# A macaron transformer layer: the context is turned by VectorE's 32x32 transposes, x1 is made as columns, and work and places move between engines

## What is computed

```python
# ffn, D=128, 16 heads of 8, 8 experts, 512 hidden
x = conv1d(x, conv_w, width 3) + conv_b
q, k, v = split(x @ wqkv.T + bqkv)
ctx = softmax(q @ k.T / sqrt(8)) @ v          # 512x512 scores for each of 16 heads
x = layernorm(x + ctx @ wo.T + bo, ln1_g, ln1_b)
probs = softmax(x @ gate_w + gate_b)          # over 8 experts
y_e = relu(x @ w1[e] + b1[e]) @ w2[e] + b2[e] # every expert on every token
x = layernorm(x + sum_e probs[e] * y_e, ln2_g, ln2_b)
# attn: per head a softmax over the 16 steps of a segment and offset of q*k, times v, then Wo
```

## Time and profile before

| | us |
|---|---|
| median of 3 runs | 1628.72 |
| lowest and highest | 1626.53 and 1637.02 |
| the profiled execution | 1626.09 |
| its span, first to last instruction | 1624.4 |
| TensorE busy | 1557.1 |
| VectorE busy | 1184.1 |
| ScalarE busy | 1151.7 |
| GpSimd busy | 981.6 |

### The profile page before, as it was taken

The page is one execution under the profiler, slowest core; times in us unless marked ns, Lnnn a source line. Parts: engine busy times, 40 slices in busy tenths (PEclk is TensorE's granted clock), DMA queues, the critical chain, the costliest instruction groups (busy, mean ns, idle before and its releaser), DMA issues.

```text
span 1624.4 us, 26990 instructions
## 1 busy us (share of the span) xinstructions
PE 1557.1 (96%) x8690; PEld 871.0 (54%) x8690; DVE 1184.1 (73%) x1885; ACT 1151.7 (71%) x1684; POOL 981.6 (60%) x925
## 2 busy tenths in 40 slices
PE   3889999999999999999999999999999999999986
PEld 2334555555555555555655555555555555555565
DVE  3766677776777778777778786878787777768365
ACT  2566777777777777677676776777677677777875
POOL 3512657676766667566675766667566676757143
PEclk7678999999999999999999999999999999999998
DMA  7533333151522424243331523425243331511111
GB/s 191 142 82 88 83 81 95 49 130 40 127 64 74 104 70 121 53 116 80 85 96 47 150 54 80 105 72 120 53 112 83 83 96 46 133 35 47 28 46 26
DMA packets 85853, 137.52 MB, mean 85 GB/s; under 512 B 8977, under 2 KB 49602, under 8 KB 81090
## 3 DMA queue, kind: packets, MB, share of 16 engines
q1 hardware_dynamic: 84434, 131.60, 31.7%
q0 software_dynamic: 1280, 4.20, 1.0%
HBM read 102.73 MB, written 32.77 MB: 83 GB/s over the span
## 4 chain that ended last, share of the span: by engine, by line
PE 82%; DVE 5%; DMA 4%; issue 3%; POOL 3%; ACT 2%; SPq 0%; POOLq 0%; DVEq 0%; ACTq 0%
PE hid_y L997 15%; PE ctx_ps L1178 14%; PE hid_y L1001 12%; PE hid_y L998 12%; PE score L1035 11%; DMA m_xn<-out 2%; PE misc L997 2%; PE misc L998 2%; PE misc L1001 2%; DVE negmax L847 1%; PE score L1055 1%; DMA f_xn<-in_L_attn_x 1%; PE misc L1102 1%; PE misc L1123 1%; PE misc L1109 1%
## 5 line engine op out<-in xcount | busy, mean ns | idle before, releaser
L559 POOL TENSOR_TENSOR hidl<-hid,hidh 128x512 fp32r<-128x512 f32 x456 | 590.2, 1309 | 342.5 <-DVE hidh L806 256.6
L847 DVE TENSOR_REDUCE negmax<-score 128x2 f32<-128x1024 f32 x484 | 590.4, 1220 | 224.9 <-PE score L1035 222.9
L673 ACT ACTIVATE probs<-score 128x1024 f32<-128x1024 f32 x468 | 480.6, 1027 | 107.3 <-PE score L1055 106.9
L702 ACT ACTIVATE hid<-hid_y,cols 128x512 f32<-128x512 f32 x484 | 332.1, 686 | 149.3 <-PE hid_y L1001 130.8
L1178 PE MATMUL ctx_ps<-probs,V 128*18 128x512 f32 x2048 | 275.6, 611 | 0.0
L1055 PE MATMUL score<-Qp,Kp 32*128 32x512 f32 (+1 forms) x1024 | 269.0, 505 | 2.6 <-ACT probs L666 2.4
L1035 PE MATMUL score<-Kp,Qp 24*128 24x512 f32 x968 | 245.1, 501 | 22.4 <-DVE negmax L847 9.5
L997 PE MATMUL hid_y<-x1h,w1h 128*128 128x512 f32 x484 | 230.9, 477 | 1.6 <-DVE negmax L847 1.3
L567 POOL TENSOR_TENSOR yacc<-yacc,gated 128x512 f32<-128x512 f32 x128 | 180.5, 1410 | 67.5 <-DVE gated L822 67.5
L699 ACT ACTIVATE hidh<-hid_y,cols 128x512 fp32r<-128x512 f32 x256 | 175.7, 686 | 51.6 <-PE hid_y L1001 49.8
L997 PE MATMUL hid_y<-hidh,w2h 128*128 128x512 f32 x512 | 206.3, 403 | 4.4 <-DVE gated L822 4.4
(11 more groups left out here) (184 smaller groups left out, 1893.1 us busy)
## 6 DMA issues: line engine op xcount, KB each, us to landing
gate_b<-gate_dram SPq DMA_DIRECT2D x128, 256.0 KB, 3.7
q_parts_dram<-q_parts SPq DMA_DIRECT2D x48, 256.0 KB, 3.0
k_parts_dram<-k_parts SPq DMA_DIRECT2D x48, 256.0 KB, 3.0
Qp<-q_parts_dram SPq DMA_DIRECT2D x64, 192.0 KB
Kp<-k_parts_dram SPq DMA_DIRECT2D x64, 192.0 KB
Qp<-q_parts_dram SPq DMA_DIRECT2D x32, 240.0 KB
Kp<-k_parts_dram SPq DMA_DIRECT2D x32, 240.0 KB
Qp<-q_parts_dram SPq DMA_DIRECT2D x32, 144.0 KB
```

Source lines behind the costliest of these rows:

```text
L559: pool.tensor_tensor(hidl[:, n % RING, :], hid[:, n % 2, :], hidh[:, n % RING, :].bitcast(F32), ALU.subtract).then_inc(s["h_lo"], 1)
L673: act.activation(probs[:, n % 2, 2 * j:2 * j + 2, :], score2[:], ACT.Exp, scale=SCALE)\
L702: act.activation(hid[:, n % 2, :], hid_bank(u, n), ACT.Relu, bias=col(n))\
L847: dve.tensor_reduce(negmax[:, g % 2, :, k % 8], banks_for_max(u.count(32, k))[:], AX.X, ALU.max, negate=True).then_inc(s["a_max"], 1)
```

## The change

Eight edits, and a new `AT`:

1. `ctx_ps` is turned by VectorE in 32x32 blocks (`dve.transpose`, one instruction per half), from PSUM to `ctxT`. Reciprocals and scaling work on `ctxT`, and one product over 256 elements takes the place of two over 128. A third `dve.transpose` turns `ctxs` back to `ctxT`. TensorE's 12 transposes and ScalarE's 3 copies go. The columns of `wo` and of the value bias are loaded in another order for it.
2. x1 is made as columns: one product with `woT` as weights and 512 columns of `ctxT`. VectorE adds the bias (now a column, `bo_col`) and `conv` in one instruction. Four transposes (`x1T`) bring it back to rows, and the moments and the centring read `misc`.
3. `yacc` is evicted by ScalarE behind `x1h`, no longer by VectorE.
4. `nm_parts` is turned by `pe.transpose`.
5. The gates are turned in one transpose of 32 columns, and stored as 32 rows of 128.
6. GpSimd centres and scales `f_xn` (units after the first) and `m_xn`, and multiplies `m_xn` by `mwt`.
7. The start loads `wo` in four pieces and the value bias in two, adds `bo2` to the columns, and drops one broadcast: five more DMAs.
8. `AT` has new places: the context's first turn from tick 56 (copy) to 59.5, `f_v` from -7 to -6, x1 from 97.5 to 93.5, the c moments from 100 to 94.5, and others by up to 5 ticks.

```diff
@@ AT
-    "f_k1": -23, "f_k2": -23, "f_qs": -24, "f_ks": -21.5, "f_v": -7, "f_vs": -7, "ctx0": 56, "ctx0T": 59.5,
-    "ctx0n": 60.5, "ctx1": 88.5, "ctx1T": 90.5, "ctx1n": 90.5, "cT": 94.5, "cTs": 94.5, "x1": 97.5, "x1p": 98,
+    "f_k": -23, "f_k1": -23, "f_k2": -23, "f_qs": -25, "f_ks": -22, "f_v": -6, "f_vs": -6, "ctx0": 59.5,
+    "ctx1": 89, "cT": 90.5, "x1": 93.5, "x1p": 92.5, "x1T": 94.5, "c_stats": 94.5, "c_centre": 95.5, "c_rs": 95,
...
@@ misc_uses
-            + [misc_use("ctx0T", "a_norm", 2, 1), misc_use("ctx1T", "a_norm", 2, 2), misc_use("cT", "c_cTs", 1, 1),
-               misc_use("x1", "c_x1p", 1, 1), misc_use("xnT", "c_x1h", 1, 1), misc_use("gate", "c_lg", 1, 1),
+            + [misc_use("x1", "c_x1p", 1, 1), misc_use("x1T", "c_cen", 1, 1), misc_use("xnT", "c_x1f", 1, 1), misc_use("gate", "c_lg", 1, 1),
...
@@ SyncE, start
-            load(wo_raw, wo, "ld_wo")
+            load(vec_rows[V_BO:V_BO + 1, :], row(bo2), "ld_vec")
+            for j in range(HG):
+                half, pair = divmod(j, 2)
+                load(wo_raw[:, 32 * j:32 * j + 32],
+                     wo[:, 64 * half:64 * half + 64].rearrange("o (g i d) -> o i g d", i=2, d=DH)[:, pair, :, :], "ld_wo")
...
@@ GpSimd
+                if T == AT["f_centre"] and u.n > 0:
+                    centre(pool, "f", u.n, f_xn)
+                if T == AT["f_norm"] and u.n > 0:
+                    normalise(pool, "f", u.n, f_xn, "f_xn")
...
+                if T == AT["m_centre"]:
+                    centre(pool, "m", b.n, m_xn)
                 if T == AT["m_rs"]:
                     inv_std("m", b.n)
+                if T == AT["m_norm"]:
+                    normalise(pool, "m", b.n, m_xn, "m_xn")
+                if T == AT["m_w"]:
+                    wait(pool, s["m_wt"], b.count(1, 1))
+                    pool.tensor_tensor(by_offset(m_xn[:]), by_offset(m_xn[:]), over_steps(mwt), ALU.mult)\
+                        .then_inc(s["m_w"], 1)
...
@@ ScalarE
-                if T in CTX_EVICT:
-                    g = CTX_EVICT[T]
-                    wait(act, s["a_pv"], u.count(16, 8 * g + 8))
-                    wait(act, s["a_ctxT"], u.count(2, g))
-                    wait(act, s["c_x1"], u.n)
-                    act.activation(ctxT[:], ctx_ps[:], ACT.Copy).then_inc(s["a_ctx"], 1)
...
-                if T == AT["cTs"]:
-                    wait(act, s["c_cT"], u.count(1, 1))
-                    act.activation(ctxT[:], misc[:], ACT.Copy).then_inc(s["c_cTs"], 1)
                 if T == AT["x1h"]:
-                    wait(act, s["c_x1f"], u.count(1, 1))
+                    wait(act, s["c_xnT"], u.count(1, 1))
...
+                    wait(act, s["e_T"], u.n - 1)
+                    act.activation(yacc[u.parity][:], misc[:], ACT.Identity, bias=col(V_B1), scale=col(V_G1))\
+                        .then_inc(s["c_x1f"], 1)
...
@@ VectorE
-                if T in CTX_NORM:
-                    g = CTX_NORM[T]
...
+                if T in CTX_TURN:
+                    g = CTX_TURN[T]
+                    wait(dve, s["a_pv"], u.count(16, 8 * g + 8))
+                    wait(dve, s["zero_ctx"], 1)
+                    wait(dve, s["c_x1T"], u.n)
+                    dve.transpose(ctxT[:], ctx_ps[:]).then_inc(s["a_ctx"], 1)
+
+                    sums = ctxT[:].rearrange("p (b r) -> p b r", r=QUARTER)[:, :, 0:2 * VC]\
+                        .rearrange("p b (l v) -> p b l v", v=VC)
+                    means = ctxs[:].rearrange("p (b t l d) -> p b t l d", t=2, l=2, d=DH)
+                    wait(dve, s["a_ctx"], u.count(2, g + 1))
+                    dve.reciprocal(rden[:], sums[:, :, :, DH]).then_inc(s["a_rden"], 1)
                     wait(dve, s["a_rden"], u.count(2, g + 1))
...
+                    dve.tensor_tensor(means[:, :, g, :, :], sums[:, :, :, 0:DH],
+                                      rden[:].unsqueeze(3).to_broadcast([128, S // QUARTER, 2, DH]), ALU.mult)\
+                        .then_inc(s["a_norm"], 1)
+                if T == AT["cT"]:
+                    wait(dve, s["a_norm"], u.count(2, 2))
+                    dve.transpose(ctxT[:], ctxs[:]).then_inc(s["c_cT"], 1)
 
                 if T == AT["x1p"]:
                     wait(dve, s["c_x1"], u.count(1, 1))
+                    wait(dve, s["set_bo"], 2)
+                    dve.scalar_tensor_tensor(out=ctxT[:], in0=misc[:], scalar=bo_col[:], in1=conv[u.parity][:],
+                                             op0=ALU.add, op1=ALU.add).then_inc(s["c_x1p"], 1)
...
@@ TensorE
-                    pe.matmul(misc[0:2 * HG * TC, 0:128], nm_parts[:].rearrange("p t a k -> p (t a k)").bitcast(F32),
-                              ident[:], start=True, stop=True).then_inc(s["a_nmT"], 1)
...
+                    pe.transpose(misc[0:2 * HG * TC, 0:128],
+                                 nm_parts[:].rearrange("p t a k -> p (t a k)").bitcast(F32), ident[:])\
+                        .then_inc(s["a_nmT"], 1)
+                if T == AT["x1"]:
...
+                    wait(pe, s["c_cT"], u.count(1, 1))
+                    pe.matmul(misc[:], woT[:], ctxT[:], start=True, stop=True).then_inc(s["c_x1"], 1)
+                if T == AT["x1T"]:
...
+                    wait(pe, s["c_x1p"], u.count(1, 1))
                     for c in range(TC):
                         last = pe.transpose(chunk(misc, c), chunk(ctxT, c), ident[:])
-                    last.then_inc(s["a_ctxT"], 1)
...
-                    for c in range(TC):
-                        pe.matmul(chunk(misc, c), chunk(ctxT, c), woT[:], start=True, stop=False)
-                        last = pe.matmul(chunk(misc, c), chunk(conv[p], c), ident[:], start=False, stop=True)
-                    last.then_inc(s["c_x1"], 1)
+                    last.then_inc(s["c_x1T"], 1)
...
-                    for c in range(TC):
-                        last = pe.transpose(misc[0:E, c * 128:(c + 1) * 128], gate[p][:, c, :], ident[:])
-                    last.then_inc(s["c_prT"], 1)
+                    pe.transpose(misc[0:TC * E, 0:128], gate[p][:].rearrange("p c e -> p (c e)"), ident[:])\
+                        .then_inc(s["c_prT"], 1)
```

More of the change, by code:

```diff
@@ L368, in _ @@
             load(vec_rows[V_CONV:V_CONV + 1, :], row(conv_b), "ld_vec")
-            load(vec_rows[V_BQ:V_BQ + 3, :], bqkv.rearrange("(a n) -> a n", a=3), "ld_vec")
+            load(vec_rows[V_BQ:V_BQ + 2, :], bqkv[0:2 * D].rearrange("(a n) -> a n", a=2), "ld_vec")
+            for half in range(2):
+                load(vec_rows[V_BV:V_BV + 1, 64 * half:64 * half + 64],
+                     bqkv[2 * D + 64 * half:2 * D + 64 * half + 64].rearrange("(g i d) -> i g d", i=2, d=DH), "ld_vec")
             for k, v in ((V_G1, ln1_g), (V_B1, ln1_b), (V_MBQ, bq), (V_MBK, bk), (V_MBV, bv)):
@@ L874, in tick @@
-                if T == AT["c_stats"]:
-                    wait(dve, s["c_x1p"], u.count(1, 1))
-                    moments("c", u.n, lambda c: chunk(x1n, c))
-                if T == AT["c_centre"]:
-                    centre("c", u.n, x1n)
-                if T == AT["c_norm"]:
-                    normalise("c", u.n, x1n, "c_xn")
-                if T == AT["x1f"]:
-                    wait(dve, s["c_xnT"], u.count(1, 1))
-                    wait(dve, s["e_T"], u.n - 1)
-                    dve.tensor_scalar(yacc[u.parity][:], misc[:], col(V_G1), col(V_B1), ALU.mult, ALU.add)\
-                        .then_inc(s["c_x1f"], 1)
+                    wait(dve, s["set_bo"], 2)
@@ new lines, in tick @@
+                    dve.scalar_tensor_tensor(out=ctxT[:], in0=misc[:], scalar=bo_col[:], in1=conv[u.parity][:],
+                                             op0=ALU.add, op1=ALU.add).then_inc(s["c_x1p"], 1)
+                if T == AT["c_stats"]:
+                    wait(dve, s["c_x1T"], u.count(1, 1))
+                    moments("c", u.n, lambda c: chunk(misc, c))
+                if T == AT["c_centre"]:
+                    wait(dve, s["e_x"], u.n - 1)
+                    centre(dve, "c", u.n, x1n, misc)
@@ L973, in mid @@
                                       ALU.mult).then_inc(s["m_wt"], 1)
-                if T == AT["m_w"]:
-                    wait(dve, s["m_wt"], b.count(1, 1))
-                    dve.tensor_tensor(by_offset(m_xn[:]), by_offset(m_xn[:]), over_steps(mwt), ALU.mult)\
-                        .then_inc(s["m_w"], 1)
                 if T == AT["m_o"]:
```

149 lines of the change are left out of this document (59 added, 90 removed).

## The result

Kernels are timed side by side. The changed kernel has a median of 1589.8 us in 4 runs (1583.9 to 1598.3), the kernel before 1632.9 (1626.5 to 1643.7): a ratio of 0.9756, 95% interval 0.9715 to 0.9797. The forecast was 1600, range 1582 to 1617.

A forecast was written before the change was run, and what follows sets the result against it. TensorE was taken as the bound, full in the steady part, with VectorE nearly failing to keep up. From the profiled 1626.1: - 43 + 12 + 1.5 + 1 = 1597.6 us, against the median 1600; range 1582 to 1617.

The forecast's parts named there:

- TensorE's saving: Fewer transposes and products on TensorE: 1.14 + 0.94 - 0.38 + 0.96 + 0.25 = 2.9 us per unit, 43 us over 15 units.
- nothing gained, or 0.96: Bounds on the gain per unit in us from turning the maxima by transposes, forecast as 4 x 0.24 = 0.96.
- The wait at the first half: At the context's first half TensorE waits for VectorE's turn, reciprocals and scaling: 0.8 us per unit, 12 us in all.
- The c norm's 1.5 us: Moments, cast and centring between two maxima, directly after x1T, make it about 0.1 us late: 15 x 0.1.
- The mids: GpSimd's three more passes in each of 8 mids were costed at nothing; without cover, up to 1.3 us each.
- the cover: GpSimd's passes are hidden because a down projection reads its `hidl` about five ticks after GpSimd's place for it.
- The start: Five more DMAs issued ahead of the rest, at 0.36 us each: at most 1.8 us, taken as 1.
- Rival 1: The wait at the first half doesn't come, because VectorE reaches it earlier: 1586 us, chance 0.22.
- Rival 2: VectorE or GpSimd later than counted (slow turns, collisions, late `m_xn`, no maxima gain): one 1608 to 1614, chance 0.25.
- Rivals 3 and 4: The third: maxima hold TensorE over the whole unit, time 1620 to 1635, chance 0.06. The fourth has its own line.
- rival 4: Slower: VectorE becomes the bound through its turns, at the second half; 1656 us for turns of 2.44, chance 0.04.
- the recorded point: Where VectorE's turns outweigh the gain: from 28 us, 1.9 per unit, that is from turns of 1.5 us on.

## Why the prediction was right, and where its terms were off

**The sum.** By the profiled executions the forecast was 28.5 us less, and 27.8 was measured. By the medians it was 28.7, and 43.1 was measured, 1.5 times as much: 1589.8 lies within the range, 10 us under the forecast. The mechanism was as forecast, less work on TensorE against a wait at the first half's turn. The close agreement of the traces is luck in two ways: they are the fastest execution of one kernel and the slowest of the other, and the terms are off in both directions.

- *TensorE's saving, 2.9 us per unit forecast, 3.27 measured.* x1 (0.85 and 0.86), its transposes (0.38 and 0.39) and the three turned halves were right. Mis-sized are the maxima: I took a quarter of four transposes, 0.10, for one, and it costs 0.02; so 4 x 0.32 = 1.28 and not 0.96, and the gates 0.31 and not 0.25. The bound that I wrote for it, "nothing gained, or 0.96", did not hold the value. The maxima and the gates were tried alone; that the turned halves and x1 give the other 1.68 us rests on the starts and on the account that closes.
- *The wait at the first half, 0.8 forecast, 0.81 measured*, with the turn at 705 ns for 0.69. But it is made otherwise: the scaling takes 0.42 us and not 0.49, and what TensorE shows is the wait for the turn at `ctx_ps`, 0.73, that I had inside a wait for the maxima. The maxima end just in time. The working has two slips that nearly cancel. Its own terms end the reduction at 730.93 + 1.53 = 732.46, not 732.6, so 0.54 and not 0.7 behind the old scores. And VectorE starts the chain 0.24 later against TensorE's scores, where I took 0.1 for the moved product: the reduction ahead of the cast ends 0.29 us before the scores at 728.91 in the earlier trace rows, and 0.05 before those at 718.15. The experiments show why an edit to one limit at this place gave nothing, and to two 0.4: behind the turn stand `gated` and the maxima, and beside them GpSimd's chain, and each takes over when the other goes; by GpSimd's hold what VectorE saves there is lost again when its cast or scaling falls inside a pass.
- *The c norm's 1.5 us* did not come: the scores from tick 30 to 32 and 32 to 34, beside and behind `x1T`, stand 2.42 and 3.01 us apart, which is 2.04 and four transposes, and the usual 3.01.
- *The mids.* I let them gain what a plain unit gains. They gained 1.7 and not 2.5. I costed GpSimd's passes at nothing, and 10 us if the cover goes. The passes are cheaper than taken (1.04 us and not 1.31, 1.53 for the weights), and taking them away makes the mids slower, not faster. The scores tell where the 0.8 goes. Some 0.4 lies between ticks 22 and 28, in every mid; 0.3 of it is a wait for `m_xn` at L1070 that the kernel before doesn't have. Some 0.3 lies between ticks 2 and 8 and is the load of `m_xn` behind `m_st`, which ranges from nothing to 2.2 us in the eight mids of this trace. The worst is one mid of 98.4 us: VectorE stands 2.9 us at `m_st` for the load of `m_xn`, TensorE 2.1 for the maxima, and its clock falls to 0.50 from 1019 to 1022 us. Rows of the timeline:

```profile
1015.58 0.88 DVE L809 BATCH_NORM_STATS2 m_st<-m_xn 128x6 f32<-128x128 f32 x4 [2.93 <-DMA m_xn<-out]
...
1016.89 1.19 DVE L865 TENSOR_REDUCE negmax<-score 128x2 f32<-128x1024 f32 x1
...
1018.14 0.50 PE L1035 MATMUL score<-Kp,Qp 24*128 24x512 f32 x2 [2.12 <-DVE negmax L865]
```

- *The start, 1 us forecast, 4.0 measured*, of which 2.7 is a wait for `wo`. The first mark differs as much between kernels that don't differ there, so I can't say how much of it is the change's.

**The rivals.** Rival 1 (no wait) fell: the wait is there in all 15 units. Rival 2 names the collision of VectorE and GpSimd. It is real, 0.38 against 1.33 us for one cast, yet in the changed kernel's order it costs nothing that the account of a plain unit would miss; it decides what a different order at that place gives. Rivals 3 and 4 fell by the starts and by the turn's 705 ns. For rival 4 the recorded point, turns of 1.5 us, doesn't follow from its own terms: 3 x 1.13 - 1.5 = 1.9 gives turns of 1.8. The runs add that it may lie lower: one turn more, 0.7 us in the first half alone, takes 1.2 of the 2.5 us in a plain unit, though little in the mids. The second half was not tested.

For the turn, the Trainium skill (Vector Engine (DVE) Microarchitecture Reference, section 3.8) has one element per cycle per lane; the trace agrees, 705 ns beside the 692 of an elementwise pass of the same size. The estimate from another page of the Trainium skill, VectorE: DVE Perf Modes (The three transpose paths), four blocks at 311 ns, 1.24 us, does not hold for one instruction over 128x512: it takes 0.57 of that.

For the cast, the Trainium skill (GPSIMD Engine Reference, Key points) has GpSimd share its SBUF interfaces with VectorE's instructions in a 2-port mode as well as with those of two SBUF inputs. The 1.33 us beside the addition and the 0.38 without it agree, though no run here shows in which mode the cast runs; the prediction had applied the rule to the scaling of the e norm alone.

## What to carry to other kernels

Price an inserted product by the starts around it, not by its record, and put one multiplication with the identity in the form of a transpose: here a record reads 289 to 291 ns in both forms, two records or one, and the cost was 0.34 or 0.02 us. When a wait vanishes and the unit keeps its length, list what is due within half a microsecond behind it, on every engine; here there were three such limits, and only moving two at once shortened a unit. Keep VectorE's casts and its multiplications with two SBUF inputs out of GpSimd's passes: look at which pass is running when each starts. And before a step is moved later, follow its store to whoever loads those rows: 0.4 us won in a plain unit became nearly 3 us lost in a unit with a mid.

## What the runs showed of the chip

- A wait of TensorE can be followed by half its clock. Of the waits from 200 to 1480 us in the traces here, all of 2.3 us and more were followed by a granted clock of 0.50 (the level of 1.2 GHz). Of the shorter ones some were and some weren't: with the turn done twice, one of 1.49 us was and one of 1.50 wasn't, and one of 2.13 in another run wasn't. In the trace after, the clock fell at 1473 behind waits of no more than 0.85 and 0.70 us, 1.2 us apart. The lower clock lasted 3 to 7 us. Beside a wait of 2.1 us two distances of scores grew by 3.7 together (4.24 and 4.52 for 2.05 and 3.01), beside one of 4.2 us one grew by 6.8. That this is what spreads the times of one kernel was not shown.
- VectorE's cast, and its multiplications with two inputs in SBUF, wait for the GpSimd pass in which they start: they end 0.28 us (a cast of 512 columns, a scaling of 256) or 0.55 us (a scaling of 512) behind it. The context's scaling, where it starts just ahead of a pass, keeps its 0.42 us and the pass is longer, 1.53 us for `hidl` and not 1.27.
- VectorE turns 128x512 float32 in 32x32 blocks in 705 ns from PSUM and 697 from SBUF.
- A float32 transpose of 32 columns, alone in a full stream of products, adds 0.02 us between starts; four of 128 columns in a row add 0.38.
- GpSimd's centring and scaling of 128x512, whose second input repeats one value along the row, takes 1.04 us, its addition of two full tiles 1.30 to 1.35.
